# A new sum of y that begins a step later, the turned orientation carried in six pieces, and two doubling DMAs a state pair earlier

## What is computed

```python
xs = concat([x_hwwh, flip(x_hwwh, -1)], 1)      # 4 directions: flat, turned, and both reversed
h = h * exp(dt * A) + (dt * u) * B              # along L = 1024 positions, N = 16 states per channel
y = einsum('bkcn,bkn->bkc', h, C)               # sum over the 16 states
y = out_y[:, 0] + inv_y[:, 0] + wh_y + invwh_y  # wh_y, invwh_y: turned back from (w, h) to (h, w)
```

## Time and profile before

| | |
|---|---|
| timed executions | 1623.06, 1631.72 and 1634.27 us; median 1631.72 us |
| profiled execution | 1635.15 us, of which the span from the first to the last instruction is 1633.4 us |
| mean granted TensorE clock | 0.947 |
| busy share of the span | TensorE 82%, VectorE 75%, GpSimd 63%, ScalarE 62% |

### The profile page before, as it was taken

How to read it: one execution, slowest core, us unless ns; L and a number is a source line. 1 busy time by engine, 2 the same in 40 slices (tenths; PEclk the granted TensorE clock), 3 DMA queues, 4 the chain that set the end, 5 groups by cost and what they waited for, 6 DMA issues and landing times. The chain is left out here.

```text
span 1633.4 us, 66391 instructions
## 1 busy us (share of the span) xinstructions
PE 1343.7 (82%) x30408; PEld 826.3 (51%) x30408; DVE 1232.6 (75%) x1025; ACT 1013.5 (62%) x1916; POOL 1025.2 (63%) x294
## 2 busy tenths in 40 slices
PE   7997779787886978788697878869786867879998
PEld 5735556444553644455364545536444534436554
DVE  4975298979898897989889798988979885732220
ACT  2458678767877876687787667778777540402222
POOL 0002189889898988989898898989889860000000
PEclk8998789999999999999999999999999997879999
DMA  9244424323233432323343232334323225101101
GB/s 331 83 160 174 121 68 111 95 70 97 68 91 74 110 98 68 97 68 91 74 111 97 67 98 68 85 80 107 95 74 113 73 68 223 39 0 39 39 29 49
DMA packets 73478, 151.08 MB, mean 92 GB/s; under 512 B 33238, under 2 KB 41942, under 8 KB 72816
## 3 DMA queue, kind: packets, MB, share of 16 engines
q1 hardware_dynamic: 73200, 146.83, 30.6%
HBM read 101.72 MB, written 32.51 MB: 82 GB/s over the span
## 5 line engine op out<-in xcount | busy, mean ns | idle before, releaser
L1193 POOL TENSOR_TENSOR s_h<-s_h,s_crow 128x2048 f32<-128x2048 f32 (+1 forms) x256 | 879.2, 3464 | 183.6 <-DVE s_h L1158 183.4
L1158 DVE TENSOR_TENSOR_SCAN s_h<-s_a,s_pb 128x1024 f32<-128x1024 f32 x384 | 865.0, 2277 | 166.5 <-PE s_pb L1002 130.8
L1002 PE MATMUL s_pb<-k_area,m_dtut 64*64 64x64 f32 x24576 | 470.2, 224 | 184.7 <-DVE s_h L1158 135.5
L1002 PEld LDWEIGHTS s_pb<-k_area,m_dtut 64*64 64x64 f32 x24576 | 427.7, 137 | 364.6 <-DVE s_h L1158 191.2
L1041 PE MATMUL s_py<-s_h,k_eye 64*64 64x512 f32 x3072 | 422.7, 604 | 21.5 <-ACT y_y L1090 15.6
L284 ACT ACTIVATE k_area<-k_mask,m_bt 128x64 f32<-128x64 f32 x992 | 274.1, 338 | 0.0
L1084 ACT ACTIVATE s_a<-y_y,m_aneg 128x1024 f32<-128x1024 f32 x192 | 218.5, 1139 | 30.0 <-DVE s_h L1158 30.0
L1084 ACT ACTIVATE s_a<-m_dup,m_aneg 128x1024 f32<-128x1024 f32 x192 | 219.4, 1143 | 26.8 <-DVE s_h L1158 26.8
L199 POOL TENSOR_TENSOR k_area<-m_bt,k_mask 128x2048 f32<-128x2048 f32 x33 | 145.6, 4412 | 127.4 <-ACT m_bt L262 127.4
L1041 PEld LDWEIGHTS s_py<-s_h,k_eye 64*64 64x64 f32 x3072 | 91.0, 136 | 36.3 <-ACT y_y L1090 16.0
L262 ACT COPY y_y<-m_pm 128x384 f32<-128x384 f32 (+1 forms) x96 | 49.2, 513 | 93.4 <-PE m_pm L219 82.0
(11 more groups left out here) (189 smaller groups left out, 1236.4 us busy)
## 6 DMA issues: line engine op xcount, KB each, us to landing
s_crow<-scratch_xd SPq DMA_DIRECT2D x256, 256.0 KB, 4.0
k_area<-in_x_dram SPq DMA_DIRECT2D x4, 1536.0 KB, 7.5
scratch_xt<-y_y SPq DMA_DIRECT2D x4, 1536.0 KB, 8.8
y_y<-y_y SPq DMA_DIRECT2D x24, 256.0 KB, 3.4
m_dup<-m_dup SPq DMA_DIRECT2D x24, 256.0 KB, 3.2
out_dram<-t_out SPq DMA_DIRECT2D x32, 192.0 KB, 1.9
k_area<-scratch_xt SPq DMA_DIRECT2D x3, 1536.0 KB, 6.8
scratch_xd<-h_dbl SPq DMA_DIRECT2D x8, 512.0 KB, 2.6
```

The lines of the kernel that those rows point to most:

```text
L1002: mm = pe.matmul(pb[par * HALF:(par + 1) * HALF, step % 2, r * BANK + blk:(r + 1) * BANK:BLK], dtut[here, u % 2, blk, g * HALF:(g + 1) * H ...
L1158: nc.vector.tensor_tensor_scan(h[:, step % (TRIPLES * CG), f], a[:, step % RING, f], pb[:, step % 2, f], 0.0, ALU.mult, ALU.add).then_inc( ...
L1193: nc.gpsimd.tensor_tensor(here, here, c.unsqueeze(1).broadcast_to([P, groups.stop - groups.start, L]), ALU.mult).then_inc(hc_ready, 1)
```

## The change

In a unit that begins a new sum (every even unit but the first) TensorE's list of sums, the new function `sums`, leaves step 7 empty; the first sum comes at step 8, and step 9 adds two, so that from step 9 on the lag is 7 again. Every new sum now opens its PSUM regions itself (`opens` no longer asks for the flat orientation). In the first turned unit the carried y is added to the open sums in six pieces at steps 10 to 15: four matmuls of 256 columns for `py`, one for each of steps 10 to 13, and two pairs for `py2` at steps 14 and 15. Each piece waits for the sum ahead of it, and the next instruction on TensorE for the piece. ScalarE's `take_y` at the batch start moves ahead of the exponents and rows of step 6. The doubling DMAs of groups 0 and 1 go to state pair 6.

```diff
+CAUGHT_UP = 9
+CARRIED = 6
...
+                    if n == 6 and u + 1 < UNITS:
+                        m.double(sp, u + 1, range(2))
                     if n == 7 and u + 1 < UNITS:
-                        m.double(sp, u + 1, range(CG))
+                        m.double(sp, u + 1, range(2, CG))
...
-            def carry(b):
-
-                for x, q in enumerate(halves()):
-                    pe.matmul(py[:, q].rearrange("p (w h) -> p w h", h=HW), eye[:],
-                              y01[:].rearrange("p (h w) -> p w h", w=HW)[:, x * HW // 2:(x + 1) * HW // 2], start=True, stop=False)
-                for apart in range(2):
+            def carry(b, piece):
+
+                first = CG * NP * 4 * b + CG * NP * 2
+                pe.wait_ge(y_added, first + CAUGHT_UP + 2 + piece - LAG)
+                if piece < 4:
+                    q, w = halves()[piece // 2], piece % 2
+                    mm = pe.matmul(py[:, q].rearrange("p (w h) -> p w h", h=HW)[:, w * HW // 4:(w + 1) * HW // 4], eye[:],
+                                   y01[:].rearrange("p (h w) -> p w h", w=HW)[:, piece * HW // 4:(piece + 1) * HW // 4],
+                                   start=False, stop=False)
+                else:
                     for x in range(2):
-                        lh = x ^ apart
+                        lh = x ^ (piece - 4)
...
-                    mm.then_inc(y_carried, 1)
-                    pe.wait_ge(y_carried, 2 * b + apart + 1)
+                mm.then_inc(y_carried, 1)
+                pe.wait_ge(y_carried, CARRIED * b + piece + 1)
...
                 if first and part == 0:
                     need(pe, y_taken, 2 * taken(b, o))
-                    if o == 1:
-                        carry(b)
...
-                    opens, closes = first and o == 0 and part == (0, 0, 1)[into], last and part == (2, 1, 2)[into]
+                    opens, closes = first and part == (0, 0, 1)[into], last and part == (2, 1, 2)[into]
...
+            def sums(u, i):
+
+                at = u * STEPS + i - LAG
+                held = u > 0 and u % 2 == 0
+                if at < 0 or held and i == LAG:
+                    return []
+                if held and LAG < i < CAUGHT_UP:
+                    return [at - 1]
+                if held and i == CAUGHT_UP:
+                    return [at - 1, at]
+                return [at]
+
             for u in range(UNITS):
                 for i in range(STEPS):
                     step = u * STEPS + i
                     spread_b(u, i)
-                    if step >= LAG:
-                        add_y((step - LAG) // CG, (step - LAG) % CG)
+                    for summed in sums(u, i):
+                        add_y(summed // CG, summed % CG)
+                    if u % 4 == 2 and CAUGHT_UP < i <= CAUGHT_UP + CARRIED:
+                        carry(u // 4, i - CAUGHT_UP - 1)
...
                     if step + AHEAD < LAST:
                         decay(step + AHEAD)
+                    if i == 6 and s == 0 and o == 0 and u:
+                        take_y(b - 1)
...
                     if i < 6:
                         m.build_rows(act, u, 2, share(i + 6), share(i + 7))
-                    if i == 6 and s == 0 and o == 0 and u:
-                        take_y(b - 1)
```

More of the change, by code:

```diff
@@ L1005, in spread_b @@
                 mm.then_inc(b_row, 1)
-            def carry(b):
-                for x, q in enumerate(halves()):
-                    pe.matmul(py[:, q].rearrange("p (w h) -> p w h", h=HW), eye[:],
-                              y01[:].rearrange("p (h w) -> p w h", w=HW)[:, x * HW // 2:(x + 1) * HW // 2], start=True, stop=False)
-                for apart in range(2):
+            def carry(b, piece):
[7 more added lines that the diff above has]
+                else:
                     for x in range(2):
-                        lh = x ^ apart
+                        lh = x ^ (piece - 4)
                         here, cols = slice(lh * HALF, (lh + 1) * HALF), slice(x * HW // 2, (x + 1) * HW // 2)
                         mm = pe.matmul(py2[x * HALF:(x + 1) * HALF].rearrange("p (w h) -> p w h", h=HW)[:, :, lh * HW // 2:(lh + 1) * HW // 2],
-                                       eye[here, here], y2[here].rearrange("p (h w) -> p w h", w=HW)[:, cols], start=(apart == 0), stop=False)
-                    mm.then_inc(y_carried, 1)
-                    pe.wait_ge(y_carried, 2 * b + apart + 1)
+                                       eye[here, here], y2[here].rearrange("p (h w) -> p w h", w=HW)[:, cols], start=False, stop=False)
+                mm.then_inc(y_carried, 1)
+                pe.wait_ge(y_carried, CARRIED * b + piece + 1)
             def add_y(n, part):
@@ L1087, in take_y @@
                 act.wait_ge(y_added, CG * NP * 4 * (b + 1))
-                act.wait_ge(y_carried, 2 * (b + 1))
+                act.wait_ge(y_carried, CARRIED * (b + 1))
                 nc.scalar.copy(y01[:].rearrange("p (h w) -> p h w", w=HW), py[:].rearrange("p (w h) -> p h w", h=HW)).then_inc(y_taken, 1)
```

## The result

Six timed executions of the changed kernel have a median of 1609.35 us (1607.35 to 1614.97), six of the kernel before 1632.99 us; the ratio is 0.9864, with a 95% interval of 0.9824 to 0.9904. By the medians that is 23.6 us less, by the ratio 22, where 35.1 were forecast: faster by 1.4% (1.0 to 1.8), and inside the range (1588 to 1612), at its upper end. The profiled execution took 1609.95 us.

A forecast was written before the change was run, and what follows sets the result against it. VectorE's scans were taken to be bound by waits for TensorE's `pb`, the long ones at the seven starts of a sum. 24.0 + 11.1 = 35.1 us off the median 1631.72 gave 1597 us, range 1588 to 1612.

The forecast's parts named there:

- The hold at the turned starts: Step 8's `spread_b` ahead of the wait for `y_taken`: scan 8 follows scan 7 at once, 24.0 us over four starts.
- The batch starts: Three batch starts: both scan waits gone, the logarithm is late next; gains 3.48, 3.98 and 3.67 us, together 11.1.
- the 2 to 3 that I gave as a sign: Batch starts: VectorE should wait 2 to 3 us for the logarithm ahead of its first `softplus`.
- ScalarE is not in the way: Batch starts: an earlier logarithm lets `softplus` follow scan 9, 6.1 instead of 3.5 us gained each; 1589 us, chance 0.10.
- The six pieces at no cost: Steps 10 to 15: TensorE's 1.49 us idle before each `spread_b` covers a piece; 0, without cover 23.7 us.
- The rival is out: Pieces show: their waits exceed TensorE's idle time and the step's lead; up to 23.7 us lost, 1597 to 1621, chance 0.16.
- GpSimd as the pacer: After each start, GpSimd's 3.67 us idle limits the gain to 25.7 us over seven starts; 1606 us, chance 0.07.
- The doublings at no cost: State pair 6: the load of C goes perhaps 5 us later, but GpSimd has 9 us in hand; cost 0.
- TensorE goes cold: Logarithm gap leaves TensorE at 1.2 GHz past step 15, 1.28 us lost a step; 72 us, 1669 us, chance 0.05.
- a place where I said I would be wrong: Signs against the forecast: low granted clock in steps 10 to 23, or another wait of about 3 us in the same units.
- The sum: Whole kernel: 24.0 us from turned starts plus 11.1 from batch starts, 35.1 us in all.
- 90: Scan stage sign: the scans' total wait for `pb` should fall from 130.8 to about 90 us.

The follow-up runs named there:

- the part alone: Hold and pieces at the four turned starts alone, batch starts and doublings as in the kernel before, against that kernel: ratio 0.9863.

## Why the prediction was right, and what it missed

*The hold at the turned starts*: right, in place and size. 5.97 us came at the first, where 5.96 were worked out from the cadence of the scans; the part alone gave 22.4 us of 24.0, within its interval (18 to 26).

*The batch starts*: right in that the logarithm takes the place of the wait, and in the size: 3.4 us at the first of 3.48 forecast. But I had both waits for scans gone, and scan 9 waits at all three. At the first start it waits 0.98 us for a `decay` that I didn't look at, which ScalarE, behind with its work, still reached only after the copies and the exponent. At the other two it waits 1.65 and 0.59 us for `spread_b`, because I had the first sum at full clock, and it wasn't (0.57 from 776 to 780 us); TensorE's timeline at the second start:

```profile
776.20 1.86 PE L1047 MATMUL s_py<-s_h,k_eye 64*64 64x512 f32 x8 [0.99 <-ACT y_y L1110]
777.81 1.95 PE L1006 MATMUL s_pb<-k_area,m_dtut 64*64 64x64 f32 x64
```

So the wait for the logarithm was 1.72, 1.42 and 1.17 us, not the 2 to 3 that I gave as a sign. Since the logarithm was due later still, all this cost nothing. The rival "ScalarE is not in the way" falls; making the logarithm early took a change of its own.

*The six pieces at no cost*: right, though a term was undersized. The matmul of a piece took 1.11 us, 1.16 with its waits, where I had 0.92 for the matmul alone; that is still inside the 1.49 us of cover, and scans 10 and 11 stand as close as before. The rival is out.

*GpSimd as the pacer*: out. It allows a gain of 25.7 us at most, and with the doublings at 7 the change brings 31.2.

*The doublings at no cost* is the step that failed. I asked only who waits for the C load, found that GpSimd had 9 us in hand, and took 0. That part holds: GpSimd didn't wait for C. But a transfer that nobody waits for still takes the DMA engines while it runs (their share went from 0.17 to 0.72 where the C load went), and beside it run transfers that are waited for. The likely ones are TensorE's instruction loads. The page before has them as a queue of their own ("instruction", 240 packets, 3.93 MB, 1.0% of the engines' time), and its list of waits has 43.2 us of TensorE waiting for "issue"; I read neither. The price is 5.9 us on the kernel before, 8.7 us on the changed one, instead of 0. That the price exists is shown; its way through the instruction loads is argued from the rhythm of the stops and from the thinned loads of C.

*TensorE goes cold*: not as the rival had it. The gap at the logarithm, 1.94 us at the first batch start, kept the full clock, 1.00 in the windows on both sides:

```profile
508.51 1.16 PE L1006 MATMUL s_pb<-k_area,m_dtut 64*64 64x64 f32 x64 [1.94 <-DVE s_h L1178]
```

```profile
502.00:506.00 4.00, 3.39 (x144) 2.68 (x135) 2.24 (x3) 4.00 (x9) 4.00 (x2) 1.00 0.82 157
506.00:512.00 6.00, 2.67 (x84) 1.25 (x80) 5.97 (x6) 4.17 (x10) 5.61 (x2) 1.00 0.34 97
```

The Trainium skill (TensorE: Matmul & The Clock Gate, section "Why this matters for your kernels") advises against idle gaps between bursts of matmuls. The trace agrees behind the stops: after the 2.92 us at u = 3 a sum took 2.02 us, and at the end of u = 14

```profile
1240.00:1244.00 4.00, 0.00 (x0) 0.00 (x0) 0.42 (x1) 1.69 (x4) 4.00 (x2) 1.00 1.00 340
1244.00:1250.00 6.00, 5.31 (x152) 3.73 (x156) 4.12 (x2) 1.87 (x4) 4.21 (x2) 0.72 0.24 57
```

TensorE stands still for four us with the DMA engines fully busy, and the stretch behind has a mean granted clock of 0.72. So these two stops are paid for twice. The second is a place where I said I would be wrong: a scan that waits over 3 us (4.80) and a low clock, in step 23. The change didn't open it: the kernel before stops for 3.85 us about there, too. In both, a load of 1536 KB that only the last unit has runs beside it.

*The sum.* By the means of the ratios, of 35.1 us the changed kernel brings 22.5, and without the doublings 31.2. Of the remaining 4 us, 0.7 are the batch starts (3.38, 3.51 and 3.57 us measured instead of 3.48, 3.98 and 3.67); the rest is within the intervals and stays open. Open is also why the scans' waits for `pb` fell to 103.1 us and not to 90: without the doublings they are 98.6 and 101.2.

That the time lies inside the range is in part luck. Its upper end was set for GpSimd and the pieces, which cost nothing; it took in a loss that the sum had at 0.

## What to carry to other kernels

Cost a moved transfer twice: by who waits for it, and by which transfers run beside it at its new place. A gap in the DMA traffic in front of a crowd may be worth keeping, and waits for "issue" in the middle of a group, at even distances in the program, hint that an engine's own instruction loads are in that crowd. When a wait is taken away, look for the next producer that was hidden behind it, here a logarithm on ScalarE 2.7 us later, ask of every input of the next instruction when it is ready, and measure the parts of a change apart: this one had a part that gave 31 us and one that cost a fifth to a quarter of that.

## What the runs showed that was not expected

TensorE's supply of instructions seems to be a cost of its own in a kernel with 30,424 matmuls: its stops lie about 127 matmuls apart, or multiples of that, and there is one instruction load per 126.8. Thinning the loads of C took the stops from 44.2 to 17.4 us and the time by 28 us; stops hit the middle of a group of matmuls that waits for no semaphore, up to 4.9 us long with the DMA engines 1.00 busy, and a stop of 2.92 us brought the lower clock behind it. A change that moves only the order of issues on the sync queue, without GpSimd ever waiting for the load that moved, made the kernel 0.36% slower.
